# A selective-scan block pipeline: ScalarE's jobs in another order (x's silu in two halves, z's silu beside the tanh, delta's quarters moved up)

## What is computed

```python
# part 1: conditioned recurrence
proj = conv(x) @ Wp + bp
B_t = softplus(proj[..., :N]); C_t = tanh(proj[..., N:])       # N = 64
state = decay * state + dt * B_t * (x @ Ws + bs); y = C_t * state; x1 = y @ Wo + bo
# part 2: Mamba block on x1
xz = layernorm(x1) @ W_in;  x_br, z = split(xz)                 # 1024 channels each
xb = silu(causal_conv4(x_br))
Bm = xb @ W_b;  Cm = xb @ W_c;  delta = softplus(xb @ W_delta + b_delta)
h = exp(delta * A) * h + delta * Bm * xb                        # 16 states a channel
y = sum_s(h * Cm) + xb * Dp
x = x + y * silu(z) @ W_out + x1
# part 3: a low-rank conditioned layer and a quantized FFN (not touched)
```

## Time and profile before

| | |
|---|---|
| median of 3 runs | 2659.27 us (2657.55 to 2660.13) |
| the profiled execution | 2653.91 us, span 2651.9 us |
| PE busy in the span | 2309.5 us (87%) |
| DVE busy | 2265.5 us (85%) |
| POOL busy | 1728.4 us (65%) |
| ACT busy | 1669.0 us (63%) |
| scan phase | up to some 2134 us, the FFN phase behind it |

### The profile page before, as it was taken

The page is one execution under the profiler, slowest core; times in us unless marked ns, Lnnn a source line. Parts: engine busy times, 40 slices in busy tenths (PEclk is TensorE's granted clock), DMA queues, the critical chain, the costliest instruction groups (busy, mean ns, idle before and its releaser), DMA issues. The chain is left out here.

```text
span 2651.9 us, 34212 instructions
## 1 busy us (share of the span) xinstructions
PE 2309.5 (87%) x11520; PEld 1586.2 (60%) x11520; DVE 2265.5 (85%) x2232; ACT 1669.0 (63%) x3332; POOL 1728.4 (65%) x2042
## 2 busy tenths in 40 slices
PE   7778889888898988888988888888888875999997
PEld 5566667676666666757666666666666322444443
DVE  2399999999999999899999999999999835888886
ACT  2567676667667676767676767676766534555554
POOL 0278787878787878778787778787878711222221
PEclk8889999999999999999999999999998987999999
DMA  4102020202010110102020202020104621111110
GB/s 186 72 1 72 9 76 6 76 5 80 16 65 21 61 53 28 65 17 73 9 72 10 72 10 72 10 76 5 72 10 189 233 83 56 60 64 66 59 52 24
DMA packets 48299, 151.74 MB, mean 57 GB/s; under 512 B 8069, under 2 KB 8965, under 8 KB 45198
## 3 DMA queue, kind: packets, MB, share of 16 engines
q1 hardware_dynamic: 48142, 149.76, 15.9%
HBM read 132.37 MB, written 17.37 MB: 56 GB/s over the span
## 5 line engine op out<-in xcount | busy, mean ns | idle before, releaser
L472 POOL TENSOR_TENSOR ring<-ring,Cbc 128x512 f32<-128x512 f32 x1024 | 1283.1, 1275 | 44.5 <-POOL carry L465 0.4
L864 DVE TENSOR_TENSOR_SCAN ring<-a_ps,ring 128x1024 f32<-128x1024 f32 x512 | 1168.0, 2281 | 106.7 <-ACT a_ps L702 105.2
L702 ACT ACTIVATE a_ps<-delta,nA 128x255 f32<-128x255 f32 x2048 | 852.9, 468 | 380.3 <-DVE ring L864 379.4
L1069 PE MATMUL yT_ps<-ident,ring 128*128 128x128 f32 x4096 | 588.1, 284 | 163.5 <-POOL ring L472 160.0
L1069 PEld LDWEIGHTS yT_ps<-ident,ring 128*128 128x128 f32 x4096 | 475.0, 145 | 282.2 <-POOL ring L472 241.9
L856 DVE TENSOR_TENSOR ring<-u_ps,Bbc 128x1024 f32<-128x1024 f32 x512 | 619.7, 1210 | 16.0 <-PE yT_ps L1069 9.3
L1035 PE MATMUL work<-xb,big 128*128 128x256 f32 x2048 | 476.8, 385 | 10.1 <-ACT zs L560 10.1
L1035 PEld LDWEIGHTS work<-xb,big 128*128 128x128 f32 x2048 | 385.5, 193 | 79.5 <-issue 16.9
L465 POOL TENSOR_TENSOR carry<-ring,half 128x4 f32<-128x4 f32 x512 | 127.1, 248 | 361.2 <-DVE ring L864 359.7
L1051 PE MATMUL work<-Wout,xb 128*128 128x512 f32 x512 | 237.7, 599 | 0.0
L1414 POOL TENSOR_TENSOR m<-m,pows 128x1 f32<-128x1 f32 x64 | 34.2, 549 | 311.4 <-DVE m L1546 311.4
(11 more groups left out here) (197 smaller groups left out, 2508.1 us busy)
## 6 DMA issues: line engine op xcount, KB each, us to landing
Bbc<-bc_rows SPq DMA_DIRECT2D x64, 512.0 KB, 4.6
Cbc<-bc_rows SPq DMA_DIRECT2D x64, 512.0 KB, 3.7
xT<-in_xT SPq DMA_DIRECT2D x16, 514.0 KB, 3.5
x_rows<-x2row SPq DMA_DIRECT2D x32, 256.0 KB, 2.0
xp<-x_rows SPq DMA_DIRECT2D x32, 256.0 KB, 2.7
xx<-in_x SPq DMA_DIRECT2D x32, 256.0 KB, 3.0
out_rows<-orow SPq DMA_DIRECT2D x32, 256.0 KB, 2.0
delta<-in_c_w SPq DMA_DIRECT2D x6, 1024.0 KB, 5.3
```

Of the source, the lines that this page charges most:

```text
L472: nc.gpsimd.tensor_tensor(hp, hp, Cbc[:, G * g + GP * c:G * g + GP * c + GP, :], ALU.mult)\
L702: r = nc.scalar.activation(a_ps[q % 2][:, i, 1:T], delta[:, par, dt, 1:T], ACT.Exp, scale=nA[:, dt, s:s + 1])
L864: dve.tensor_tensor_scan(ring[:, q % RING, :, :].rearrange("p g t -> p (g t)"), a_ps[q % 2][:, :, :].rearrange("p g t -> p (g t)"), ring[: ...
L1069: r = pe.matmul(yT_ps[:, tt, :], ring[:, q % RING, i, P * tt:P * tt + P], ident[:, :], is_transpose=True, start=False, stop=(g == NG - 1 a ...
```

## The change

ACT's plan of slots is written anew. x's silu is done in two halves, slots 15 and 17, each with its own switch to silu's table and back. The Exp of part 1 moves from slot 5 to slot 4 and its Ln from slot 6 to slot 5; behind it a new job, visit, switches to silu's table, runs the Tanh and both halves of z's silu (of the block that is about to be scanned, where before z's silu ran in slot 30 for the next block), and switches back. delta's second quarter dexp(1) and zcopy(2) move from slot 27 to 26, dln(0) from 28 to 27. keep_y0 moves from DVE to ACT. DVE's gates0 moves from slot 4 to 3.

```diff
@@ prj, prj_ln, visit, keep_y0 on ACT
+                    wait(act, s_c0, 6 * n)
                     nc.scalar.activation(e0[:, :], ps[0:N0, 0:T], ACT.Exp, bias=sc0[0:N0, 4:5]).then_inc(s_e0, 1)
-                    wait(act, s_c0, 6 * n)
-                    nc.scalar.activation(c0[:, :], ps[N0:P, 0:T], ACT.Tanh, bias=sc0[N0:P, 4:5]).then_inc(s_tanh, 1)
                 def prj_ln():
-                    nc.scalar.preload_act_table_set("natural_log_exp_and_others")
                     act.wait_ge(s_c0, 6 * n + 1)
                     nc.scalar.activation(e0[:, :], e0[:, :], ACT.Ln, bias=1.0).then_inc(s_l0, 1)
+                def visit():
+                    nc.scalar.preload_act_table_set("silu_and_others")
+                    if front:
+                        nc.scalar.activation(c0[:, :], work[BANK["PRJ"]][N0:P, 0:T], ACT.Tanh, bias=sc0[N0:P, 4:5])\
+                            .then_inc(s_tanh, 1)
+                    if scan:
+                        zsilu(k, par)
+                    nc.scalar.preload_act_table_set("natural_log_exp_and_others")
+                def keep_y0():
+                    if back:
+                        act.wait_ge(full[BANK["WOUT1"]], jobs_before("WOUT1", k) + 1)
+                    act.wait_ge(s_c0, 6 * n + 5)
+                    nc.scalar.activation(y0k[:, fp, :], y0[:, :], ACT.Copy).then_inc(s_c0, 1)
@@ silu on ACT
-                def silu():
-                    for j in (ND // 2 - 2, ND // 2 - 1):
+                def silu(i):
+                    for j in (2 * i, 2 * i + 1):
                         act.wait_ge(free[BANK[f"XB{j}"]], jobs_before(f"XB{j}", k) + 1)
-                    for i in range(2):
-                        v = xb[:, fp, 4 * i:4 * i + 4, :].rearrange("p a b -> p (a b)")
-                        nc.scalar.activation(v, v, ACT.Silu).then_inc(s_xb, 1)
+                    v = xb[:, fp, 4 * i:4 * i + 4, :].rearrange("p a b -> p (a b)")
+                    nc.scalar.activation(v, v, ACT.Silu).then_inc(s_xb, 1)
                     nc.scalar.preload_act_table_set("natural_log_exp_and_others")
@@ ACT's slots, two lines of the table
-                             17: [lambda: xcopy(3), silu], 20: [bc], 21: [lambda: zcopy(0)], 23: [lambda: zcopy(1)],
+                             26: [lambda: zcopy(2), lambda: dexp(1, False)],
@@ the loop over slots on ACT, behind the plan's jobs
+                    if q == 5 and (front or scan):
+                        visit()
@@ DVE
-                next_plan = {4: [gates0], 5: [scan0], 13: [keep_y0]}
+                next_plan = {3: [gates0], 5: [scan0]}
```

More of the change, by code:

```diff
@@ L644, in rowcopy @@
                     nc.scalar.activation(xw[:, c % 2, :], work[0][0:2, :], ACT.Copy).then_inc(s_rowcp, 1)
-                next_plan = {5: [prj], 6: [prj_ln], 8: [lambda: stats(0)], 9: [lambda: stats(1)], 10: [y0scale],
-                             11: [y0back], 14: [lambda: xcopy(0)], 15: [lambda: xcopy(1)], 16: [lambda: xcopy(2)],
-                             17: [lambda: xcopy(3), silu], 20: [bc], 21: [lambda: zcopy(0)], 23: [lambda: zcopy(1)],
-                             25: [lambda: dexp(0, False)], 27: [lambda: zcopy(2), lambda: dexp(1, False), lambda: dtail(0, False)],
-                             28: [lambda: zcopy(3), lambda: dln(0, False)], 30: [lambda: zsilu(n, fp)],
+                next_plan = {4: [prj], 5: [prj_ln], 8: [lambda: stats(0)], 9: [lambda: stats(1)], 10: [y0scale],
+                             11: [y0back], 13: [keep_y0], 14: [lambda: xcopy(0)], 15: [lambda: xcopy(1), lambda: silu(0)],
+                             16: [lambda: xcopy(2)], 17: [lambda: xcopy(3), lambda: silu(1)], 20: [bc],
+                             21: [lambda: zcopy(0)], 23: [lambda: zcopy(1)], 25: [lambda: dexp(0, False)],
+                             26: [lambda: zcopy(2), lambda: dexp(1, False)],
+                             27: [lambda: dtail(0, False), lambda: dln(0, False)], 28: [lambda: zcopy(3)],
                              31: [lambda: dexp(2, False)]}
                 if isinstance(k, int) and k == -1:
-                    next_plan.update({27: [lambda: dexp(1, False), lambda: dtail(0, False)],
-                                      28: [lambda: dln(0, False), lambda: zcopy(2), lambda: zcopy(3)], 30: [], 31: []})
+                    next_plan.update({26: [lambda: dexp(1, False)], 28: [lambda: zcopy(2), lambda: zcopy(3)], 31: []})
                 scan_plan = {2: [lambda: dexp(3, True), lambda: dtail(1, True)], 6: [lambda: dln(1, True)]}
@@ L659, in step @@
                     scan_plan[1] = [lambda: dexp(2, True)]
-                    scan_plan[3] = [lambda: zsilu(k, par)]
                 turned = {13: 0, 20: 1, 28: 2}
@@ L772, in scan0 @@
                     dve.memset(mark[:, :], 0.0).then_inc(free[BANK["PRJ"]], 1)
-                def keep_y0():
-                    if back:
-                        dve.wait_ge(full[BANK["WOUT1"]], jobs_before("WOUT1", k) + 1)
-                    dve.wait_ge(s_c0, 6 * n + 5)
-                    dve.tensor_copy(y0k[:, fp, :], y0[:, :]).then_inc(s_c0, 1)
                 def mx_scale():
```

## The result

The changed kernel takes **2704.57 us** (median of 4 runs, 2703.55 to 2704.97); the kernel before, run beside it, takes 2659.42 (4 runs, 2657.55 to 2660.13). The ratio is 1.017, with an interval of 1.0153 to 1.0188: slower by 45 us. The forecast was slower, by 21.

The account below looks back on a forecast made before the run. DVE was taken as the bound, waiting mostly on ACT's exponentials (105.2 us). Terms -1.0, +1.6 and +1.2 gave +1.8 us a block, +25 over 14 blocks, +21 with the ends: 2680 us, range 2664 to 2700.

Parts of the forecast that it names:

- Term A: Slots 14 to 17, x's silu in halves: scan 17 about 1.0 us earlier, -1.0 us a block.
- Term B: Slots 25 to 31, delta and block end: scan 31 +2.3, u product -0.7, so +1.6 us a block (1.2 to 2.5).
- that run moves with scan 27: Slots 27 to 31: PE's 7.07 us run holding dl(2) shifts with scan 27 (+2.7), putting scan 31 2.3 later.
- Term C: Slots 3 to 10, tanh and z's silu: late gT(3) delays PE's WOUT products, +1.2 us a block (0.6 to 2.1).
- the middle: WOUT products after slot 5: shift taken as 1.16, between 0.6 with PE's clock back and 2.1 with it low.
- The edges: Outside the 14 blocks: -1 us in the prologue, about -3 in the first block, where z's silu leaves slot 3.
- Slower by twice as much: Clock low in wout(0,0), u product just behind a GpSimd half's start: +3.6 us a block, 2706 us; chance 0.12.
- No change: Slots 3 to 10: PE makes late gT(3) good, -0.65 there, 0 a block, 2655 us with the ends; chance 0.12.
- Faster: Slot 26: z(2) 3.57 us sooner, no new wait there; -3.2 us a block, 2610 us; chance 0.13.
- Loads at twice the price: Slots 5 and 15: a moved table load costs twice today's, engine emptied around it; +130 us, 2790 us; chance 0.03.

Follow-up runs that it names:

- e1: Kernel before with only x's silu in two halves (slots 15 and 17, two more table loads a block): 2643.11 us, 0.9939 of the kernel before.
- e2: Changed kernel with the copy gT(3) moved from slot 6 to the start of slot 5, ahead of the logarithm and the visit: 2656.11 us, 0.9987.
- e3: Changed kernel with zcopy(2), dexp(1), dtail(0) and dln(0) back in slots 27 and 28, as before the change: 2656.04 us, 0.9982.
- e5: Changed kernel with x's silu whole again in slot 17, four table loads a block instead of six: 2707.82 us, 1.0194.
- e10: As e8, with 16 fillers in place of 4 behind the turn of slot 3, filling most of PE's pause: 2677.81 us, 1.0072.
- e7: Changed kernel with zcopy(3) moved from slot 28 to the head of slot 27: 2751.95 us, 1.0363.
- e4: Changed kernel with the edits of e2 and e3 together: 2617.05 us, 0.9847 of the kernel before.
- e8: Changed kernel with four additional unread PE transposes (fillers) behind the turns of slots 1, 2 and 3 each: 2703.12 us, 1.016.
- e6: Changed kernel with three additional unread PE transposes at the end of the turn of slot 3, in PE's pause: 2700.32 us, 1.0163.

## Why the forecast had the direction and half the size

**Term A, forecast -1.0, measured -0.96.** Right in size and mechanism: the waits came out at 1.02 and 1.83 (forecast 1.2 and 1.9), and e1 shows the term by itself. The two further loads in slot 15 cost only the wait in slot 15. The Trainium skill ("ScalarE: Activation LUTs", section "What ACT_TABLE_LOAD costs") adds a drain about as long as the load itself; the trace does not agree here, with 1.28 a load, the silu 0.01 behind its end, and 40 us for 32 loads in e1.

**Term B, forecast +1.6, measured +2.1.** The step of the sum was right: 3.49 in slot 26 (forecast 3.57), none in 27 and 30, the u product 0.85 (forecast 1.0); and e2, whose blocks do not alternate, measures +1.48. What was off is the sentence "that run moves with scan 27": it moves by the forecast 2.7 in the short blocks, but in every second block the eight matmuls ahead of it are at the slow level, it starts 1.3 later, and scan 31 comes 1.2 later (1.6 from the block's first scan, 123.13 and 124.77 in odd and even blocks, of which 0.4 is term C's). That this belongs to PE and not to ACT the two windows and dl's rows show. e3 takes PE's idle time down to 0.62, and the eight take 2.0 in every block. e2 and e5 leave it at 3.3 and end the alternation all the same, at 2.0 (2.4 once) and at 2.8 to 3.3.

**Term C, forecast +1.2, measured +2.43: the step that failed.** The mechanism was right, and its size was not: the text had PE's clock in the late products between its two ends, 0.6 with the clock back and 2.1 with the clock low, and "the middle" had no row behind it. It stayed low through nearly all six, and they took 1.2 longer. The row that should have decided was there: the clock was at 0.50 in this very stretch before the change, and the change added idle time to it. The delay itself was right (2.2 against the forecast 2.1), and so, nearly, were the ends: e10, with the clock at 1.00, measures 0.70, and the changed kernel 2.43, over the upper one. In the forecast's own sum, 2.2 of delay and 1.2 of clock less 0.9 of slack make 2.5. The largest of the waits, 1.78, stands already in slot 7, at the turn of the Bbc rows, and not at the product for slot 10 from which the text worked the term out.

**The edges, forecast -4, measured about 0.** The way to the first scan gave 3.8 and not 1. In the first block I counted the silu that leaves slot 3 (-3) and forgot that this block has slots 26 to 31 too, so that term B stands against it: +0.25. The last block I did not price; it is 4.1 longer, with a wait for PE in slot 9 that is the changed kernel's longest on that row:

```profile
2089.94 1.23 DVE L863 TENSOR_TENSOR ring<-u_ps,Bbc 128x1024 f32<-128x1024 f32 x1 [3.13 <-PE yT_ps L1076]
```

These three were only read from the trace; no run took them apart. With gT(3) first (e2) the last block is still 3.7 longer than before, so the late copy does not make most of it, and its cause stays open.

The error of 28 us against the span (49.3 - 21) is thus 14 x 1.2 of C = 17, 14 x 0.5 of B = 7, and 4 of the edges. The range had an error of its own: with B and C at their ends the sum gives 2666 to 2706, and the text took 2664 to 2700.

**The rivals.** "Slower by twice as much" is what happened, for the first of its two reasons (the slow clock in wout(0,0)) and not the second: the u product met GpSimd at a good moment, and what B has over the forecast is the slow clock at dl(2), which no rival named. "No change" fails on its own condition, since PE did not make the late copy good. "Faster" needed z(2) earlier, and its copy starts 3.3 behind scan 25, where it started 3.2 behind it before. Loads at twice the price fall with e1.

**What stays open.** Why the clock falls at dl(2) in one block and not in its neighbour, after the same 3.3 us of idle time. Since whether it does is not told by the length of the pause, I could not have priced it from one block. e7's 47 us were read as clock and path, and the alternation from the rows of dl(2); no run with fillers at either place confirmed it.

## What to carry to other kernels

A copy that another engine waits for must not be queued behind a clump: one copy of 0.60 us, moved by one line of a table (e2), was worth 48 us, while the clump itself (tanh and z's silu with two loads) cost nothing that the table shows where it was put. So when a stretch of ScalarE is reordered, list for each instruction in it who waits for its result, and move those ahead; then look at PE's granted clock in the row where its wait grows, and price the matmuls behind a longer pause at the level that the clock has there, not at a mean of both. A slow stretch of PE is free as long as it has slack, and is paid in full once a late copy has used the slack up. The order of e4 keeps what the change was good for (2617 us, 1.5% under the kernel before) and leaves the copies that PE and the scans wait for where they were, or ahead of it.

## What the runs showed of the hardware

- In e8 the clock was 1.00 up to the end of a pause of 1.82 us and 0.53 in the 3 us behind it. With 12 more fillers in the pause, 0.52 of it left (e10), it stayed at 1.00. Those matmuls compute nothing, and they are worth 1.7 us a block, 24 us in 14. In the changed kernel itself the clock had fallen already ahead of the pause (0.67 in 1029 to 1031). The Trainium skill ("TensorE: Matmul & The Clock Gate", section "HAM oscillation — how this bites in real kernels") says that a stream of matmuls cut by waits is throttled anew at each piece; this trace agrees that waits of PE bring it, here once in each block, at 0.50 over the products of slot 5.
- The same pause had either outcome: 3.29 us before dl(2) with the clock at 1.00 behind it, and 3.30 with 0.55, in turn from block to block.
- Three fillers in the pause, with 1.15 of it left (e6), and twelve ahead of it (e8) brought nothing in the blocks; filling the pause as well (e10) did.
- What a low clock costs depends on the place. 2.0 us more in dl's run (7.07 to 9.04), for which scan 31 waits, show there as a wait of 4.06 (e7). 1.78 more in the eight matmuls of the changed kernel come out as 1.2 at scan 31, and 0.8 to 1.3 more in e5 as 0.1. The six matmuls of slot 5 took 1.0 more in blocks 1 to 4 of the kernel before than in the others and cost nothing.
- A table load cost its 1.28 us of ACT and no more: 32 more of them made ACT busy for 40 us more, in a kernel that is 0.6% faster (e1).
